# Linear attention's gate as two narrow products per chunk instead of one multiplied weight

## The reference, cut to what matters

```python
x = x + _L0_attn_a_ref(_layernorm(x), ...)
x = x + _L0_ffn_ref(_layernorm(x), ...)          # three cycles of a small gelu network
x = x + _L0_attn_b_ref(_layernorm(x), ...)       # linear attention, below
x = x + _L0_ffn_ref(_layernorm(x), ...)

def _L0_attn_b_ref(x, Wq, Wk, Wv, Wo, Wg1, Wg2, ln_w, ln_b):
    q = silu(x @ Wq); k = silu(x @ Wk); v = x @ Wv      # 256 x 256 each
    q, k = rope(split(q)), rope(split(k))               # 16 heads of 16
    energy = einsum('bhnd,bhmd->bhnm', q, k) * tril
    out = einsum('bhnm,bhmd->bhnd', energy, v)
    gate = sigmoid(x @ Wg1 @ Wg2)                       # Wg1 256 x 16, Wg2 16 x 256
    out = out * gate
    return (layernorm(out) * ln_w + ln_b) @ Wo
```

## Time and profile before

| | us |
|---|---|
| runs shown, median of 3 | 2079.09 (2078.86 to 2079.82) |
| the profiled execution: its own time | 2074.16 |
| the profiled execution: span from the first to the last instruction | 2072.3 |

### The profile page before, as it was taken

How to read it: one execution, slowest core, us unless ns; L and a number is a source line. 1 busy time by engine, 2 the same in 40 slices (tenths; PEclk the granted TensorE clock), 3 DMA queues, 4 the chain that set the end, 5 groups by cost and what they waited for, 6 DMA issues and landing times.

```text
span 2072.3 us, 47390 instructions
## 1 busy us (share of the span) xinstructions
PE 1970.2 (95%) x14758; PEld 791.0 (38%) x14758; DVE 1807.6 (87%) x3350; ACT 1493.8 (72%) x2955; POOL 199.5 (10%) x442
## 2 busy tenths in 40 slices
PE   7899999999999999999999999989897889998995
PEld 4323333333333333333333333334433555665432
DVE  7899999999999999999999999955447788877358
ACT  5358888888888888888888888855546655545757
POOL 2300000000000000000000000041013111112012
PEclk9879999999999999999999999999999999999998
DMA  5431211221221122122112112122000000000002
GB/s 160 124 101 50 72 55 43 67 62 43 56 72 46 46 71 56 43 65 65 43 51 72 50 44 70 49 92 88 1 1 1 2 2 2 2 2 2 1 1 82
DMA packets 110205, 101.25 MB, mean 49 GB/s; under 512 B 52240, under 2 KB 91424, under 8 KB 110096
## 3 DMA queue, kind: packets, MB, share of 16 engines
q1 hardware_dynamic: 110096, 99.92, 17.7%
HBM read 78.79 MB, written 20.77 MB: 48 GB/s over the span
## 4 chain that ended last, share of the span: by engine, by line
PE 85%; DVE 8%; ACT 4%; issue 2%; DMA 1%; POOL 0%; SPq 0%; ACTq 0%; DVEq 0%; POOLq 0%
PE ps L694 24%; PE ps L669 16%; PE ps L717 11%; PE ps L723 11%; PE ps L830 5%; PE ps L839 3%; PE ps L944 3%; PE ps L953 2%; PE ps L683 2%; PE ps L1026 1%; PE ps L635 1%; PE ps L614 1%; PE ps L993 1%; DVE mx L1514 1%; PE ps L973 1%
## 5 line engine op out<-in xcount | busy, mean ns | idle before, releaser
L1514 DVE TENSOR_REDUCE mx<-ps 128x1 f32<-128x512 f32 x2048 | 1272.8, 682 | 10.8 <-PE ps L669 5.5
L1123 ACT ACTIVATE YT<-ps 128x512 f32<-128x512 f32 x2048 | 1056.5, 603 | 254.6 <-PE ps L723 254.6
L694 PE MATMUL ps<-YT,work 128*32 128x512 f32 x4096 | 546.1, 605 | 0.0
L669 PE MATMUL ps<-work 64*128 64x512 bf16 x2048 | 455.3, 389 | 6.3 <-DVE mx L1514 5.0
L717 PE MATMUL ps<-work 64*128 64x512 bf16 x2048 | 394.7, 378 | 0.1
L723 PE MATMUL ps<-work 34*128 34x512 bf16 x2048 | 393.8, 378 | 0.0
L669 PEld LDWEIGHTS ps<-work 64*128 64x128 bf16 x2048 | 144.7, 93 | 610.6 <-DVE mx L1514 537.1
L717 PEld LDWEIGHTS ps<-work 64*128 64x128 bf16 x2048 | 143.3, 94 | 84.0 <-ACT YT L1123 16.8
L723 PEld LDWEIGHTS ps<-work 34*128 34x128 bf16 x2048 | 100.5, 94 | 77.4 <-issue 1.1
L694 PEld LDWEIGHTS ps<-YT,work 128*32 128x32 f32 x4096 | 80.7, 108 | 120.3 <-ACT YT L1123 112.8
L839 PE MATMUL ps<-work,c_s 128*128 128x512 f32 x192 | 97.5, 633 | 14.9 <-ACT work L1190 9.7
(11 more groups left out here) (186 smaller groups left out, 1815.1 us busy)
## 6 DMA issues: line engine op xcount, KB each, us to landing
work<-k_scr SPq DMA_DIRECT2D x640, 64.0 KB, 2.1
work<-q_scr SPq DMA_DIRECT2D x640, 32.0 KB, 1.7
o_scr<-o_sb SPq DMA_DIRECT2D x32, 256.0 KB, 2.1
X<-in_L_attn_a_x_dram SPq DMA_DIRECT2D x8, 512.0 KB, 6.9
work<-negt SPq DMA_DIRECT2D x256, 1.0 KB
work<-o_scr SPq DMA_DIRECT2D x16, 256.0 KB
work<-inv_scr SPq DMA_DIRECT2D x16, 256.0 KB
out_dram<-X SPq DMA_DIRECT2D x8, 512.0 KB, 2.9
```

The costliest lines, as they stand in the source:

```text
L669: mm(ps[:, bank_of[x], :], qa[rows, p, jp, qt * P:(qt + 1) * P], ka[rows, p, kc_ * CH:(kc_ + 1) * CH], start=True, stop=True).then_inc(a_m ...
L694: m = mm(ps[32 * j:32 * j + 32, 7, :], vst[:, p, t, :], prob(GROUP * t + j), start=t == 0, stop=t == KTILES - 1)
L1123: fn(prob(u), ps[:, S_BANK + u % S_RING, :], ACT.Exp, scale=HD ** -0.5).then_inc(exp_ok, 1)
L1514: dve.tensor_reduce(mx[:, p, at_:at_ + 1], ps[:, bank_of[x], :], AX_X, ALU.max).then_inc(a_max, 1)
```

## The change

The weight `Wg1 @ Wg2` is no longer made: `gate_turn`, `gate_product`, their copies on ACT and PE's wait for `w_gs` are gone from `feed_forward(0)`. The value product per tile has 256 columns instead of 512 (`project_vg`). The gate is made per chunk of four tiles, in two products.

The first (`gate_columns(c)`, ahead of the value product of the last tile before the chunk) multiplies `g1_s`, padded with zeros from 16 to 32 columns, by the four tiles of 128 tokens; tile i of the chunk goes to partitions 32 i to 32 i + 31 of bank 1. That is 8 matmuls of 32 weight columns and 128 moving columns. ACT copies the result to `g_t` (128 x 128). The second (`gates(c)`, after `attend` of the chunk's first tile) multiplies the 16 rows of each tile by `g2_s`, which is now held four times, at partitions 0, 32, 64 and 96; the four results of 256 columns go to banks 3 to 6. ACT takes one tanh over all four (128 x 1024) into `gate`. The next `energy`, and a `turn_chunk` in the same step, wait for that tanh (`l_gate`), since they write those banks. `gates(c)` itself waits until ACT has read bank 3 for the next tile (`l_kt`, `l_qx`, `l_qt`). Three more DMAs load the copies of `g2_s`, and DVE clears the padding of `g1_s` at the start.

```diff
-        lvg_s = sb("lvg_s", [P, KT, 2 * DIM])
-        g1_t = sb("g1_t", [HD, KT, P])
+        lv_s = sb("lv_s", [P, KT, DIM])
-        g1_s = sb("g1_s", [P, KT, HD])
-        g2_s = sb("g2_s", [HD, DIM])
+        g1_s = sb("g1_s", [P, KT, 32])
+        g2_s = sb("g2_s", [P, DIM])
+        gate = sb("gate", [P, 4, DIM])
...
+            *((g2_s[32 * i:32 * i + HD, :], g2) for i in range(4)),
...
+        def opened_by(n):
+
+            if n == 0:
+                return 0
+            return (n + 1) // 4 if (n + 1) % 4 == 0 and n + 1 < TILES else None
...
-                def gate_turn():
-
-                    pe.wait_ge(f_ga, 3)
-                    for kt in range(KT):
-                        m = pe.transpose(ps[0:HD, 7, kt * P:(kt + 1) * P], g1_s[:, kt, :], ident[:])
-                    m.then_inc(w_gt, 1)
-
-                def gate_product():
-
-                    pe.wait_ge(w_ge, 1)
-                    for kt in range(KT):
-                        m = mm(ps[:, 7, kt * DIM:(kt + 1) * DIM], g1_t[:, kt, :], g2_s[:], start=True, stop=True)
-                    m.then_inc(w_gm, 1)
-
...
-                    if k == 0 and n == GLOBAL_AT[1] - 2:
-                        gate_turn()
-                    if k == 0 and n == GLOBAL_AT[1] - 1:
-                        gate_product()
-                        pe.wait_ge(w_gs, KT)
...
+            def gate_columns(c):
+
+                pe.wait_ge(n_y, 2 * (2 * NCH + c + 1))
+                pe.wait_ge(consts, 5)
+                for kt in range(KT):
+                    for i in range(4):
+                        tok = c * CH + i * P
+                        mm(ps[32 * i:32 * i + 32, 1, DIM:DIM + P], g1_s[:, kt, :], YT[:, kt, tok:tok + P],
+                           start=kt == 0, stop=kt == KT - 1, skip_group_check=True)
+
             def project_vg(n, p):
 
                 wait(pe, l_v, n)
-                wait(pe, l_gate, n)
+                wait(pe, l_gt, opened(n))
                 wait(pe, l_x, n - 3)
+                if opened_by(n) is not None:
+                    gate_columns(opened_by(n))
                 for kt in range(KT):
-                    m = mm(ps[:, 1, :], y_st8[:, p, kt, :], lvg_s[:, kt, :], start=kt == 0, stop=kt == KT - 1)
+                    m = mm(ps[:, 1, 0:DIM], y_st8[:, p, kt, :], lv_s[:, kt, :], start=kt == 0, stop=kt == KT - 1)
                 m.then_inc(l_vg, 1)
+
+            def gates(c):
+
+                pe.wait_ge(l_gt, c + 1)
+                pe.wait_ge(l_kt, 4 * c + 2)
+                pe.wait_ge(l_qt, 4 * c + 2)
+                pe.wait_ge(l_qx, 4 * c + 2)
+                for i in range(4):
+                    own = slice(32 * i, 32 * i + HD)
+                    mm(ps[:, 3 + i, 0:DIM], g_t[own, :], g2_s[own, :], start=True, stop=True).then_inc(l_g, 1)
...
                 pe.wait_ge(l_qx, n + 1)
                 wait(pe, l_em, 4 * n)
+                wait(pe, l_gate, (n + 3) // 4)
...
                     attend(n, p, n % TPB == 0)
+                    if n % 4 == 0:
+                        gates(n // 4)
                 if n - 2 in MOMENTS_AT:
+                    if n % 4 == 0:
+                        pe.wait_ge(l_gate, n // 4 + 1)
                     turn_chunk(2, MOMENTS_AT[n - 2])
...
-                wait(act, l_r, n - 1)
-                fn(gate[:, p, :], ps[:, 1, DIM:2 * DIM], ACT.Tanh, scale=0.5).then_inc(l_gate, 1)
+                if opened_by(n) is not None:
+                    wait(act, l_g, 4 * opened_by(n))
+                    act.copy(g_t, ps[:, 1, DIM:DIM + P]).then_inc(l_gt, 1)
+
+            def gates(c):
+
+                act.wait_ge(l_g, 4 * (c + 1))
+                wait(act, l_r, 4 * c)
+                fn(gate[:], ps[:, 3:7, 0:DIM], ACT.Tanh, scale=0.5).then_inc(l_gate, 1)
...
-                dve.wait_ge(l_gate, n + 1)
+                dve.wait_ge(l_gate, n // 4 + 1)
```

More of the change, by code:

```diff
@@ L149, in hybrid_block @@
             (last_c[0:64, 1:2], e3),
-            (lqk_s[:, :, 0:DIM], tiled(lq)), (lqk_s[:, :, DIM:2 * DIM], tiled(lk)), (lvg_s[:, :, 0:DIM], tiled(lv)),
-            (lo_s[:], tiled(lo)), (g1_s[:], tiled(g1)), (g2_s[:], g2),
+            (lqk_s[:, :, 0:DIM], tiled(lq)), (lqk_s[:, :, DIM:2 * DIM], tiled(lk)), (lv_s[:], tiled(lv)),
+            (lo_s[:], tiled(lo)), (g1_s[:, :, 0:HD], tiled(g1)),
+            *((g2_s[32 * i:32 * i + HD, :], g2) for i in range(4)),
             (cos_s[:], cos_in.rearrange("(t p) e -> p t e", p=P)),
@@ L257, in hybrid_block @@
         rt = take(4, 2 * HEADS, HD // 2)
-        gate, v_x = take(2, DIM), take(2, HEADS, 32)
+        g_t, v_x = take(4, P)[:, 0], take(2, HEADS, 32)
         k_t, q_t = take(2, KT, P), take(2, KT, P)
@@ L284, in hybrid_block @@
             nm_hi nm_low nm_t m_ld qk_mm exp_ok pv_mm o_ev v_st den_ld den_inv inv_st o_norm o_mm
-            o_res w_gt w_ge w_gm w_gs f_csum f_sum f_g f_ga f_cb f_h1 f_a1 f_h2 f_a2 f_h3 f_a3 f_z f_th f_cs f_tw f_up f_out f_as f_d z_st f_pre f_pa f_co f_ze f_c3 f_cm f_mx f_u f_v
-            l_par l_vz l_ys l_qk l_vg l_silu l_v l_gate l_rt l_rope l_t l_kt l_qt l_qx l_e l_em
+            o_res f_csum f_sum f_g f_ga f_cb f_h1 f_a1 f_h2 f_a2 f_h3 f_a3 f_z f_th f_cs f_tw f_up f_out f_as f_d z_st f_pre f_pa f_co f_ze f_c3 f_cm f_mx f_u f_v
+            l_par l_vz l_ys l_qk l_vg l_silu l_v l_gt l_g l_gate l_rt l_rope l_t l_kt l_qt l_qx l_e l_em
             l_o l_s l_sx l_oe l_ot l_r l_bn l_mv l_ve l_rs l_n l_y l_ye l_w l_x
@@ L292, in hybrid_block @@
          nm_hi, nm_low, nm_t, m_ld, qk_mm, exp_ok, pv_mm, o_ev, v_st, den_ld, den_inv, inv_st, o_norm, o_mm,
-         o_res, w_gt, w_ge, w_gm, w_gs, f_csum, f_sum, f_g, f_ga, f_cb, f_h1, f_a1, f_h2, f_a2, f_h3, f_a3, f_z, f_th, f_cs, f_tw, f_up, f_out, f_as, f_d, z_st, f_pre, f_pa, f_co, f_ze, f_c3, f_cm, f_mx, f_u, f_v,
-         l_par, l_vz, l_ys, l_qk, l_vg, l_silu, l_v, l_gate, l_rt, l_rope, l_t, l_kt, l_qt, l_qx, l_e, l_em,
+         o_res, f_csum, f_sum, f_g, f_ga, f_cb, f_h1, f_a1, f_h2, f_a2, f_h3, f_a3, f_z, f_th, f_cs, f_tw, f_up, f_out, f_as, f_d, z_st, f_pre, f_pa, f_co, f_ze, f_c3, f_cm, f_mx, f_u, f_v,
+         l_par, l_vz, l_ys, l_qk, l_vg, l_silu, l_v, l_gt, l_g, l_gate, l_rt, l_rope, l_t, l_kt, l_qt, l_qx, l_e, l_em,
          l_o, l_s, l_sx, l_oe, l_ot, l_r, l_bn, l_mv, l_ve, l_rs, l_n, l_y, l_ye, l_w, l_x,
@@ L353, in is_tile, with opened @@
             return 0 <= m < TILES
+        def opened_by(n):
+            if n == 0:
+                return 0
+            return (n + 1) // 4 if (n + 1) % 4 == 0 and n + 1 < TILES else None
+        def opened(n):
+            return sum(1 for m in range(max(n, 0)) if opened_by(m) is not None)
         def through_tiles(eng, visit):
@@ L1022, in out_proj @@
                 pe.wait_ge(l_v, shown)
-                pe.wait_ge(l_gate, shown)
+                pe.wait_ge(l_gt, opened(shown))
                 wait(pe, l_x, n)
@@ L1162, in global_net @@
                         fn(gth[:, b:b + 1], ps[:, 7, 0:1], ACT.Tanh, bias=half_b[:, 1:2], scale=0.5).then_inc(f_ga, 1)
[L1164 to L1171, removed]
                 def first(n):
@@ L1241, in feed_forward @@
                         coupled(n + 2)
[L1242 to L1245, removed]
                 if k == 0:
@@ L1408, in _ @@
             dve.memset(w4_s[64:P, 0:1], 0.0).then_inc(consts, 1)
+            dve.memset(g1_s[:, :, HD:32], 0.0).then_inc(consts, 1)
             dve.memset(vals[:, :, :, HD:32], 1.0).then_inc(v_ones, 1)
@@ L1751, in gated @@
             def gated(n, p):
-                dve.wait_ge(l_gate, n + 1)
+                dve.wait_ge(l_gate, n // 4 + 1)
                 dve.wait_ge(l_ot, n + 1)
-                dve.scalar_tensor_tensor(out=o_r[:, p, :], in0=gate[:, p, :], scalar=1.0, in1=ps[:, 0, 0:DIM],
+                dve.scalar_tensor_tensor(out=o_r[:, p, :], in0=gate[:, n % 4, :], scalar=1.0, in1=ps[:, 0, 0:DIM],
                                          op0=ALU.add, op1=ALU.mult).then_inc(l_r, 1)
```

## The result

The changed kernel is slower. Over 16 runs of each it takes 2082.47 us in the median (2079.55 to 2085.82), the kernel before 2078.11 (2074.25 to 2079.82): a ratio of 1.0023 with a 95% interval of 1.0015 to 1.0031, 4.8 us. The forecast was 1.7 us less than before.

The account below looks back on a forecast made before the run. Linear attention was taken as bound by a loop of energy, masks, gated product and L944, with PE and DVE tied. Terms -8.3 + 0 + 6.6 = -1.7 us gave 2077.4 us from 2079.09, no change; forecast's own range 2074 to 2082.

Parts of the forecast that it names:

- term 3: Linear attention, `gates` in steps 0, 4, ..., 28: products on the loop between L944 and energy add 6.6 us.
- term 2: Linear attention, 32 narrower value products: PE work falls by 27.5 us but turns into waiting, so 0 us.
- Term 1: First feed-forward block: the gate's weight no longer made, so PE's wait for ACT's copies goes, -8.3 us.
- The rule on mode changes: Gate products in `gates`: tiling-mode change drains the engine; if paid per visit, 0.68 instead of 0.58 us, term 3 0.8 larger.
- Rival A: Linear attention: PE is the bound, 20 unwaited steps give 0.86 us each, total 2060 us; chance 3%.
- D: First feed-forward block: the stall moves on to another wait, Term 1 only -2.3, sum +4.3, 2083.4 us; chance 6%.
- B: Gate's cost mostly hidden, or clock gains (feed-forward end's fall may not come): sum -6, 2073 us; chance 23%.
- Rival C: Linear attention: longer idle times ahead of L944 let the clock fall; four falls give +5.1, 2084.2 us; chance 7%.

Follow-up runs that it names:

- gates_behind_turn: Changed kernel with the second gate products and their tanh moved behind `turn_chunk` in steps 4 and 16 only; 2078.72 us, ratio 0.9995.
- before_moved_wait: Kernel before, with the gate's weight made at items 10 and 11 of the first feed-forward block instead of 6 and 7; 2070.09 us, ratio 0.9963.
- tanh_one_tile: Changed kernel with ACT's gate tanh over one tile instead of four, three of four gates left out; 2082.69 us, ratio 1.0010.
- after_no_gates: Changed kernel without the second gate products, their tanh and the waits for it, the gate a constant; 2071.74 us, ratio 0.9972.

## Why the prediction was wrong

Two terms failed: term 3 was too small by 2.7 us, and term 2 put the clock at nothing.

- **Term 1, -8.3:** right. By itself -8.5 in the medians, and 8.1 in the rows of the changed kernel.
- **Term 2, narrower product, 0:** right for the loop (8.22 against 8.23 us), wrong in leaving the clock to a rival. The longer idle time was known, and its price was put at nothing in the sum. It measures 6.0 us in the profile of the changed kernel. In the timed runs it is +2.5 in the medians of the experiment, which is not clear of noise.
- **Term 3, gates, +6.6:** the other step of the prediction that failed, by size. It measures 10.3 in the profile and 10.7 in the timed pair with and without it. Both count step 0 in full. In the prediction's own count, where steps -1 and 0 are taken together, the profile gives 9.3. Four places make the 2.7 us: the four plain steps 0.90 each for 0.66 (1.0 us in all); steps 4 and 16 2.13 for 1.88 (0.5); step 8 0.57 for 0.2 (0.4); and step 0, set to 0 (0.8). There I let 2.4 us of the first two value products pay for the gates. The kernel without gates shows that steps -1 and 0 gain only 1.3 us (12.56 and 6.95 against 13.54 and 7.27), and the gates cost 2.15 (9.10 against 6.95).
- **Why a plain step costs 0.90:** 0.04 is the tanh and 0.64 the products. The remaining 0.2 stands ahead of them: they start 0.25 us after ACT's copy ends (1813.21 + 0.39 to 1813.86), not 0.10 as assumed. Energy follows the end of a tanh by 0.15 us, so the copy alone does not account for it. **The rule on mode changes,** weighed beside term 3, may: the 0.64 us lies between the 0.58 and the 0.68, but what stands ahead of the products can be part of the change of form as well. No run separates the two.
- **Sum by the timed runs:** -8.5 (stall), +2.5 (narrow product), -0.9 (columns, not told from 0), +10.7 (gates): +3.8. These are differences of neighbouring medians, so they add up to the whole by construction and do not test it; the pairs that their intervals separate are the stall and the gates.
- **Rival A** (PE is the bound): refuted by 8.22 us, **D:** refuted. The clock part of **B** came: no fall at the end of the feed-forward block in this profile.
- **Rival C,** at 7%, is half of what happened. Four falls at 1.5 us, as it had it, in steps 5, 8, 11 and 17. I weighted it by the 1.69 us waits that leave the clock high and the single 2.88 us one; the new waits of 2.54 lie between, and the lengthening was known exactly. That was not a 7% case. The kernel before had a better row for it. I had written that PE was idle for 4.45 us before the clock fell (item 8), but the clock fell inside that wait, which began at 1498.35 (columns as in the earlier trace rows):

```profile
1498.40:1500.80 2.40, 0.00 (x0) 0.00 (x0) 1.03 (x1) 2.40 (x5) 0.00 (x0) 1.00 0.00 0
1500.90:1502.70 1.80, 0.00 (x0) 0.00 (x0) 0.00 (x0) 1.80 (x4) 0.00 (x0) 0.50 0.00 0
```

PE had then been idle for about 2.5 us, which is what the narrower product was going to make of four waits. The Trainium skill (TensorE: Matmul & The Clock Gate, HAM oscillation) describes idle gaps between bursts of matmuls that bring back the half clock. The trace agrees in direction: 0.97 in the changed kernel against 1.00 with the idle time filled.

What stays open: how many falls a timed run has, and so how much of the 4.4 us between the medians is the clock. The runs of the changed kernel spread over 6.3 us, those before over 5.6; only profiled ones were seen.

## What to carry to other kernels

When a chain that ends last shows one engine at 85%, look for the second chain of the same length before pricing a shorter product on it; in a tie the saving turns into idle time, and here an idle time of PE of 2.5 us cost the stretch behind it 1.5 us of clock in most places. Work that is moved from beside the loop into it (here four products and a tanh between `attend` and `energy`) costs its full length in a plain step (0.90 us), and more where something behind it feeds another engine (2.13 us); place it where that engine has other work (0.2 us in `gates_behind_turn`). A wait for a buffer shared by two rare uses (bank 7) can be worth more than the arithmetic that it belongs to, and the wait goes away by moving one of the uses.

## What the runs showed of the hardware that I had not expected

The length of one wait does not decide whether the clock falls. In the kernel with the narrow product, waits of 2.54 us ahead of L944 were followed by a fall in steps 5, 11 and 17 (10.6 us to the next L944) and not in step 14 (9.15), and the longest, 2.89 us in step 8, was not. In `before_moved_wait` one of 2.04 us was (step 8: 10.62 us instead of the 9.14 of the kernel before, which has the same wait there). In `tanh_one_tile` one of 1.77 us was, in step 14:

```profile
1753.35 3.55 PE L936 MATMUL ps<-lqk_s,work 128*128 128x512 f32 x4 [1.77 <-DVE work L1772]
```

Four other profiles have the same 1.77 us ahead of the same product, which then takes 1.95 or 1.96 us. Of all the waits of 2.54 us ahead of this product, 14 of 18, in five profiles, were followed by a fall. The end of the first feed-forward block, where these kernels have the same code, shows it too: behind waits of 2.58 and 0.87 us two groups of L836 take 3.41 and 1.96 us in the changed kernel, and 3.78 and 3.75 in `after_no_gates`. The first L936 then comes 2.3 us later, counted from the start of the block, with nothing changed in the program.

The first feed-forward block starts anywhere within 4.1 us (1432.96 to 1437.07 over nine profiles), and within 3.2 us in the three profiles that have the same code up to there; the whole effect is 4.4 us. The length of a step repeats to the second decimal, though: every plain step from step 20 on that does not begin a chunk takes 8.22 or 8.23 us in the seven profiles without a doubled product.
